# Every second chunk's narrow one-hot on ScalarE, and counts evicted one strip later, in a graph network's counting stage

## The chip, the cores and the metric

The kernel runs on one core of a Trainium2 chip. The metric is the device time of one execution in microseconds (us). Three runs of the kernel before gave 6667.44, 6668.77 and 6669.37 us; the time before is their median, 6668.77 us.

## The reference, cut to what matters

Four graph networks (GIN, SuperGAT, a GCN/GRU chain of four blocks and an edge-filtered update) run one after the other over 3125 nodes and 100000 edges, each followed by a residual sum and a layer norm. The edges are sorted by destination. The part that matters here is the first network's sum over neighbours, which the third network uses again:

```python
edge_index = jnp.stack([src, dst])

def _gin_conv(x, src, dst, W1, b1, W2, b2):
    agg = jax.ops.segment_sum(x[src], dst, num_segments=N_NODES)
    h = x + agg
    h = jnp.maximum(h @ W1 + b1, 0.0)
    return h @ W2 + b2
```

The kernel doesn't gather rows for this. It builds a dense matrix of counts once (how many edges go from node s to node d, plus one on the diagonal for the `x +`), and multiplies by it.

## The kernel before, in words

**The counting stage** is `build_counts`. Nodes are padded to 3200, in 25 tiles (`NT`) of 128; a tile of destinations is cut into 4 strips (`PER`) of 32 destinations (`WIN`), 100 strips in all. Edges come in chunks of 128 and steps of two chunks. For strip w, `bounds` (lines 187 to 190) loads two register values from SBUF: the first step and the end of the steps that touch this strip. Since a step on the border of two strips is done in both, there are 490 steps, so 980 chunks; most strips have 5 steps.

For each chunk VectorE (DVE) makes two one-hot matrices: `pick_lo` (line 250), 128 edges by 128, marks the low 7 bits of the source; `pick_key` (line 251), 128 edges by 800, marks the pair of source tile and destination within the strip. TensorE (PE) multiplies them (line 280): `pick_lo` is the stationary side, `pick_key` the moving one, in two matmuls of 416 and 384 columns, which add into an accumulator in PSUM. Both one-hots have two buffers (b = 0 and 1, the first and second chunk of a step). DVE waits at line 249's `used` until PE has done the chunk two before; PE waits for `picked`. Around a strip PE opens the accumulator with a product of zeros (line 274) and closes it with another (line 284, semaphore `closed`). There are two accumulators; line 273 (`moved`) lets PE open one only when ScalarE (ACT) has evicted the strip two before. ACT evicts a closed strip with two copies (line 261), in the order of the strips, and does nothing else in this stage.

**GpSimd (POOL) has other work in the same block.** It sorts edge rows for the last network (class `Sender`, lines 1656 to 1702): for each tile of the counts it sends 22 chunks by indirect DMA (line 1688), in two halves of 11, each with a copy of the indices (line 1681) and a load of the next rows (line 1670). After its 22 sends, `tile` (lines 206 to 211) waits until all four strips of the tile are evicted (`moved`), and adds the identity to the diagonal block (line 211). The next tile's sends come behind it. A stage ends when all engines have come to its end: `Mem.clear` has barriers, and the next stage (`gin_conv`) begins behind them.

All engines run their own instruction streams, in order, with loops made by `Fori`; the loops over steps have bounds in registers.

Of the kernel before, what the change touches and what calls it, by code (L numbers as in the profile page):

```python
# [12 lines left out]
P = 128  # L13
N_NODES = 3125
NT = -(-N_NODES // P)
# [10 lines left out]
WIN = 1 << WIN_BITS  # L26
NWIN = NP // WIN
PER = P // WIN
# [15 lines left out]
ALU = mybir.AluOpType  # L44
ACT = mybir.ActivationFunctionType
AX_X = mybir.AxisListType.X
ds = bass.ds
# [112 lines left out]
def build_counts(nc, K, D, AT):  # L160

    with ExitStack() as ctx:
        m = Mem(nc, ctx)
        dst = m.sb("b_dst", [P, NC], I32)
        src = m.sb("b_src", [P, NC], I32)
        bits = m.sb("b_bits", [P, NC], I32)  # L170
        lof = m.sb("b_lof", [P, NC + 4 * NWIN])
        keyf = m.sb("b_keyf", [P, NC + 4 * NWIN])
        base = m.sb("b_base", [P, NWIN])
        lane = m.sb("b_lane", [P, KEYS], I16)
        lanef = m.sb("b_lanef", [P, KEYS])
        pick_lo = m.sb("b_pick_lo", [P, 2, P], BF16)
        pick_key = m.sb("b_pick_key", [P, 2, KEYS], BF16)
        zeros = m.sb("b_zeros", [P, BANK], BF16)
        sender = Sender(m, D, "b", *COUNT_SENDS)
        acc = [m.ps(f"b_acc{s}", [P, 2, BANK]) for s in range(2)]  # L180
        loaded, ready, picked, used, closed, moved, diag = (
            m.sem(f"b_{n}") for n in ("loaded", "ready", "picked", "used", "closed", "moved", "diag"))
        halves = ((0, 0, KEYS_L), (1, KEYS_L, KEYS))
        real = slice(2 * NWIN, 2 * NWIN + NC)
        flat = AT[:, :, :].rearrange("p j d -> p (j d)")

        def bounds(eng, w):
            lo = eng.value_load(K["bounds"][0:1, ds(w, 1)], min_val=0, max_val=NSTEP + NWIN)
            hi = eng.value_load(K["bounds"][0:1, ds(w + 1, 1)], min_val=1, max_val=NSTEP + NWIN)
            return lo, hi  # L190

        with nc.Block() as block:
            @block.sync
            def _(sp):
                sp.dma_start(dst[:, :], D["dst_pc"]).then_inc(loaded, 16)
                sp.dma_start(src[:, :], D["src_pc"]).then_inc(loaded, 16)

            @block.gpsimd
            def _(pool):
                pool.iota(lanef[:, :], pattern=[[1, KEYS]], base=0, channel_multiplier=0,  # L200
                          allow_small_or_imprecise_dtypes=True).then_inc(ready, 1)
                pool.iota(base[:, :], pattern=[[KEYSPAN, NWIN]], base=0, channel_multiplier=0,
                          allow_small_or_imprecise_dtypes=True).then_inc(ready, 1)
                sender.begin(pool)

                def tile(t, first):
                    sender.send(pool, t, 0, first)
                    sender.send(pool, t, 1)
                    pool.wait_ge(moved, t * (2 * PER) + 2 * PER + 2)
                    block_ = flat[:, ds(t * (NP + P), P)]  # L210
                    pool.tensor_tensor(block_, block_, K["identb"][:, :], ALU.add).then_inc(diag, 1)
                tile(0, True)
                with pool.Fori(1, NT) as t:
                    tile(t, False)
                pool.wait_ge(diag, NT)
                sender.end(pool)

            @block.vector
            def _(dve):
                dve.memset(zeros[:, :], 0.0)  # L220
                dve.drain().then_inc(used, 2)
                dve.wait_ge(ready, 2)
                dve.tensor_copy(lane[:, :], lanef[:, :])
                dve.wait_ge(loaded, 32)
                dve.tensor_scalar(bits[:, :], src[:, :], P - 1, None, ALU.bitwise_and)
                dve.drain()
                dve.tensor_copy(lof[:, real], bits[:, :])
                dve.drain()
                dve.tensor_scalar(bits[:, :], src[:, :], P_BITS, None, ALU.arith_shift_right)
                dve.drain()  # L230
                dve.tensor_scalar(keyf[:, real], bits[:, :], float(WIN), None, ALU.mult)
                dve.drain()
                dve.tensor_scalar(bits[:, :], dst[:, :], WIN - 1, None, ALU.bitwise_and)
                dve.drain()
                dve.tensor_tensor(keyf[:, real], keyf[:, real], bits[:, :], ALU.add)
                dve.drain()
                dve.tensor_scalar(bits[:, :], dst[:, :], WIN_BITS, None, ALU.arith_shift_right)
                dve.drain()
                dve.scalar_tensor_tensor(out=keyf[:, real], in0=bits[:, :], scalar=float(KEYSPAN), in1=keyf[:, real],
                                         op0=ALU.mult, op1=ALU.add)  # L240
                dve.drain().then_inc(ready, 1)
                with dve.Fori(0, NT) as t:
                    for q in range(PER):
                        w = dve.snap(t * PER + q)
                        lo, hi = bounds(dve, w)
                        with dve.Fori(lo, hi) as n:
                            for b in range(2):
                                c = dve.snap((n - w + NWIN) * 2 + b)
                                dve.wait_ge(used, n * 2 + b + 1)
                                dve.tensor_scalar(pick_lo[:, b, :], lane[:, 0:P], lof[:, ds(c, 1)], None, ALU.is_equal)  # L250
                                dve.tensor_scalar(pick_key[:, b, :], lane[:, :], base[:, ds(w, 1)], keyf[:, ds(c, 1)],  # L251
                                                  ALU.add, ALU.is_equal).then_inc(picked, 1)

            @block.scalar
            def _(act):
                act.sem_inc(moved, 2)
                with act.Fori(0, NT) as t:
                    for q in range(PER):
                        act.wait_ge(closed, t * PER + q + 1)
                        for h, lo, hi in halves:  # L260
                            act.activation(AT[:, lo // WIN:hi // WIN, ds(t * P + q * WIN, WIN)],
                                           acc[q % 2][:, h, 0:hi - lo].rearrange("p (j d) -> p j d", d=WIN),
                                           ACT.Copy).then_inc(moved, 1)

            @block.tensor
            def _(pe):
                pe.wait_ge(ready, 3)
                with pe.Fori(0, NT) as t:
                    for q in range(PER):
                        w = pe.snap(t * PER + q)  # L270
                        lo, hi = bounds(pe, w)
                        pe.wait_ge(moved, w * 2)
                        for h, a, z in halves:
                            pe.matmul(acc[q % 2][:, h, 0:z - a], zeros[:, 0:P], zeros[:, 0:z - a],
                                      start=True, stop=False, skip_group_check=True)
                        with pe.Fori(lo, hi) as n:
                            for b in range(2):
                                pe.wait_ge(picked, n * 2 + b + 1)
                                for h, a, z in halves:
                                    mm = pe.matmul(acc[q % 2][:, h, 0:z - a], pick_lo[:, b, :], pick_key[:, b, a:z],  # L280
                                                   start=False, stop=False, skip_group_check=True)
                                mm.then_inc(used, 1)
                        for h, a, z in halves:
                            mm = pe.matmul(acc[q % 2][:, h, 0:z - a], zeros[:, 0:P], zeros[:, 0:z - a],
                                           start=False, stop=True, skip_group_check=True)
                        mm.then_inc(closed, 1)
# [1819 lines left out]
```

## Time and profile before

| what | value |
|---|---|
| median of three runs | 6668.77 us |
| the profiled execution's own time | 6675.19 us |
| its span | 6673.6 us |
| busy in the span: PE, DVE, ACT, POOL | 4334.3, 3767.7, 1205.4, 3659.2 us |
| counting stage, from 151 to 1019 us | 13% of the span |

The sums and the range below are made on differences from the profiled execution, which took 6675.19 us, 1.6 us more than its span and 6.4 us (0.1%) more than the median. In the rows, times are in us from the span's start; "x2" is the number of instructions merged into a row; what stands in brackets is the idle time of the engine before the row and the engine and line that ended it. A name with a q (DVEq, ACTq, PEldq) is an engine's sequencer: register, load and branch instructions, which are not counted as busy.

### The profile page before, as it was taken

How to read it: one execution, taken by the hardware profiler on the slowest of the kernel's cores; microseconds unless marked ns; L12 is line 12 of the kernel's file. 1: busy time of each engine (PE TensorE's matmuls, PEld its weight loads, DVE VectorE, ACT ScalarE, POOL GpSimd, SP SyncE). 2: the span in 40 equal slices, each digit the busy share in tenths (PEclk: the TensorE clock that was granted, in tenths of full speed). 3: DMA queues.
4: the chain of work that ended last, by engine and by line, in shares of the span. 5: the costliest groups of instructions: out<-in, count | busy, mean ns of one | idle time of the engine just before them, and what ended most of it. 6: DMA issues, size and time to landing. Idle time of an engine off the chain costs nothing. (4 is left out here: it accounts for less than half of the span.)

```text
span 6673.6 us, 101944 instructions
## 1 busy us (share of the span) xinstructions
PE 4334.3 (65%) x26966; PEld 3026.4 (45%) x26967; DVE 3767.7 (56%) x8412; ACT 1205.4 (18%) x2011; POOL 3659.2 (55%) x3721
## 2 busy tenths in 40 slices
PE   0666667186267777775466666641888778778774
PEld 0111114154156566553355555531555556556653
DVE  8777771054589898988466666662111244444443
ACT  0111111011211111111212211110211222222221
POOL 1666664600277777772477777735000057777771
PEclk9999998598589899987577777766998888888886
DMA  4111114110244444443233333353000123222344
GB/s 198 41 44 44 41 44 177 46 33 15 64 127 116 123 122 121 117 123 75 74 81 80 79 80 83 82 114 130 11 18 21 31 64 75 74 75 74 75 71 42
DMA packets 309188, 518.20 MB, mean 78 GB/s; under 512 B 105621, under 2 KB 221727, under 8 KB 298934
## 3 DMA queue, kind: packets, MB, share of 16 engines
q0 software_dynamic: 131616, 291.86, 18.6%
q1 hardware_dynamic: 177430, 224.82, 10.3%
q8 instruction: 43, 0.70, 0.0%
q14 instruction: 99, 0.81, 0.0%
HBM read 412.95 MB, written 103.45 MB: 77 GB/s over the span
## 5 line engine op out<-in xcount | busy, mean ns | idle before, releaser
L1017 POOL DMA_INDIRECT e_ring<-att_rows,e_near x1792 | 1841.6, 1028 | 550.2 <-issue 484.2
L1770 POOL DMA_INDIRECT e_nodes<-x,e_edges x880 | 884.2, 1005 | 311.5 <-issue 274.5
L1084 PE MATMUL e_psum<-e_ring,e_whole_pick 128*128 128x264 f32 (+1 forms) x3584 | 849.5, 390 | 297.8 <-DVE e_ring L1244 288.8
L1084 PEld LDWEIGHTS e_psum<-e_ring,e_whole_pick 128*128 128x128 f32 x3584 | 649.4, 225 | 423.5 <-issue 195.7
L1039 PE MATMUL e_px<-t_parts,e_pick 128*128 x5376 | 692.9, 270 | 118.1 <-DVE e_prod L1162 56.3
L1162 DVE TENSOR_TENSOR e_prod<-e_px,e_ring 128x512 f32<-128x512 f32 x672 | 458.3, 682 | 495.9 <-DMA e_ring<-att_rows,e_near 413.3
L1688 POOL DMA_INDIRECT sorted<-bx_held,bx_index x550 | 545.0, 991 | 251.3 <-issue 248.9
L280 PE MATMUL b_acc<-b_pick_key,b_pick_lo 128*128 128x416 bf16 (+1 forms) x1960 | 504.4, 346 | 176.5 <-DVE b_pick_key L251 159.5
L350 PE MATMUL r_pa<-gru_counts,gru_parts 128*128 x3000 | 448.7, 316 | 187.3 <-DMA r_bh<-in_gru_bh 169.6
L1039 PEld LDWEIGHTS e_px<-t_parts,e_pick 128*128 128x128 bf16 x5376 | 452.6, 107 | 210.2 <-issue 139.5
L1126 ACT ACTIVATE e_whole_pick<-e_pturn 128x512 f32<-128x512 bf16 x448 | 266.5, 595 | 1324.8 <-PE e_pturn L1075 1280.5
L251 DVE TENSOR_SCALAR b_pick_key<-b_lane,b_base,b_keyf 128x800 bf16<-128x800 int16 x980 | 487.4, 497 | 0.0
L1806 PE MATMUL e_pa<-e_msg,e_pick 128*128 128x128 f32 x1768 | 315.6, 333 | 249.4 <-DVEq L1864 248.4
L1806 PEld LDWEIGHTS e_pa<-e_msg,e_pick 128*128 128x128 f32 x1768 | 264.4, 229 | 435.4 <-DVEq L1864 420.4
L350 PEld LDWEIGHTS r_pa<-gru_counts,gru_parts 128*128 128x128 bf16 x3000 | 306.7, 103 | 328.9 <-issue 193.5
L1152 DVE TENSOR_REDUCE e_dots<-e_prod 128x8 f32<-128x512 f32 (+1 forms) x672 | 453.0, 674 | 0.0
L350 PE MATMUL g_pa<-gin_counts,g_parts 128*128 x2250 | 319.6, 306 | 191.8 <-ACT g_parts L316 160.6
L1244 DVE TENSOR_TENSOR e_ring<-e_ring 128x1024 f32<-128x1024 f32 (+1 forms) x448 | 423.7, 946 | 23.7 <-issue 23.7
L250 DVE TENSOR_SCALAR b_pick_lo<-b_lane,b_lof 128x128 bf16<-128x128 int16 x980 | 264.6, 270 | 239.1 <-PE b_acc L280 194.8
L1761 POOL IOTA e_lane<- 128x128 f32 x1 | 0.2, 237 | 712.2 <-ACTq L1822 712.2
L1863 DVE TENSOR_TENSOR e_msg<-e_msg,e_nodes 128x512 f32<-128x512 f32 x220 | 153.7, 699 | 397.3 <-DMA e_nodes<-x,e_edges 395.9
L280 PEld LDWEIGHTS b_acc<-b_pick_key,b_pick_lo 128*128 128x128 bf16 x1960 | 121.5, 98 | 543.5 <-DVE b_pick_key L251 527.7
(335 smaller groups left out, 6579.9 us busy)
## 6 DMA issues: line engine op xcount, KB each, us to landing
e_relb<-place SPq DMA_DIRECT2D x56, 1024.0 KB
sorted<-o_fill SPq DMA_DIRECT2D x13, 2244.0 KB, 34.3
e_edges<-sorted SPq DMA_DIRECT2D x221, 132.0 KB
e_ring<-att_rows,e_near POOLq DMA_INDIRECT x1792
kept<-gin_counts SPq DMA_DIRECT2D x5, 4000.0 KB, 33.5
gru_counts<-kept SPq DMA_DIRECT2D x5, 4000.0 KB
bx_held<-in_edge_rows POOLq DMA_DIRECT2D x51, 363.0 KB
e_nodes<-x,e_edges POOLq DMA_INDIRECT x880
```

Of the source, the lines that this page charges most:

```text
L251: dve.tensor_scalar(pick_key[:, b, :], lane[:, :], base[:, ds(w, 1)], keyf[:, ds(c, 1)], ALU.add, ALU.is_equal).then_inc(picked, 1)
L280: mm = pe.matmul(acc[q % 2][:, h, 0:z - a], pick_lo[:, b, :], pick_key[:, b, a:z], start=False, stop=False, skip_group_check=True)
L350: mm = pe.matmul(banks, parts[:, k, j, f * P:(f + 1) * P], AT[:, j, ds(g * GW + half * HW, HW)], start=(j == 0 and k == 0), stop=(j == NT ...
L1017: pool.indirect_dma_start(out=ring[:, s, r, 0:wd + HEADS], out_offset=None, in_=xrows, in_offset=bass.IndirectOffsetOnAxis(ap=near[:, s, r ...
L1039: mm = pe.matmul(px[g % 2][:, x * wd:(x + 1) * wd], pick[:, 1 - s, r, :], parts[:, n, ds(t, 1), :].rearrange("p o c -> p (o c)"), start=(n ...
L1084: mm = pe.matmul(psum[q % 2][:, 0:RING], whole_pick[:, q % 2, c, :], ring[:, s, q * G + c, :], start=(c == 0), stop=(c == G - 1))
L1152: dve.tensor_reduce(dots[:, s, :, g * XB:(g + 1) * XB].rearrange("p h x -> p x h"), prod[:, g % 4, :].rearrange("p (x h c) -> p x h c", x= ...
L1162: dve.tensor_tensor(prod[:, g % 4, :].rearrange("p (x c) -> p x c", x=XB), px[g % 2][:, :].rearrange("p (x c) -> p x c", x=XB), ring[:, 1 ...
L1244: dve.tensor_tensor(rows_, rows_, ring[:, s, q * G:(q + 1) * G, wd:wd + HEADS].unsqueeze(3).broadcast_to([P, G, HEADS, ch]), ALU.mult).the ...
L1688: pool.indirect_dma_start(out=self.D["sorted"], in_=self.held[s][:, u, :], in_offset=None, out_offset=bass.IndirectOffsetOnAxis(ap=self.in ...
L1770: pool.indirect_dma_start(out=nodes[:, s, u, :], out_offset=None, in_=source, in_offset=bass.IndirectOffsetOnAxis(ap=edges[:, q, u, RBF + ...
L1806: mm = pe.matmul(pa[s][:, 0:P], pick[:, s, u, :], msg[:, s, u, :], start=(u == 0), stop=(u == SUB - 1))
```

## The change

DVE keeps making `pick_key` for both chunks of a step and `pick_lo` for the first one. The `pick_lo` of the second chunk is made by ACT with two activations: the absolute difference of the lane number and the source's low bits, into a new f32 tile `away`, and then relu(1 - that). ACT waits for its own first result (`away_made`), for `used`, and at the end of each step for its own second result (`placed`). PE waits for `placed` as well before the second chunk. ACT now loads the bounds of each strip and loops over its steps. The eviction of a strip comes behind ACT's work for the next strip, in place of right after the strip was closed; the last one comes behind everything.

```diff
+        away = m.sb("b_away", [P, P])
...
                             for b in range(2):
                                 c = dve.snap((n - w + NWIN) * 2 + b)
                                 dve.wait_ge(used, n * 2 + b + 1)
-                                dve.tensor_scalar(pick_lo[:, b, :], lane[:, 0:P], lof[:, ds(c, 1)], None, ALU.is_equal)
+                                if b == 0:
+                                    dve.tensor_scalar(pick_lo[:, b, :], lane[:, 0:P], lof[:, ds(c, 1)], None, ALU.is_equal)
                                 dve.tensor_scalar(pick_key[:, b, :], lane[:, :], base[:, ds(w, 1)], keyf[:, ds(c, 1)],
                                                   ALU.add, ALU.is_equal).then_inc(picked, 1)
...
             def _(act):
                 act.sem_inc(moved, 2)
-                with act.Fori(0, NT) as t:
-                    for q in range(PER):
-                        act.wait_ge(closed, t * PER + q + 1)
-                        for h, lo, hi in halves:
-                            act.activation(AT[:, lo // WIN:hi // WIN, ds(t * P + q * WIN, WIN)],
-                                           acc[q % 2][:, h, 0:hi - lo].rearrange("p (j d) -> p j d", d=WIN),
-                                           ACT.Copy).then_inc(moved, 1)
+                act.wait_ge(ready, 3)
+
+                def place(t, q):
+
+                    w = act.snap(t * PER + q)
+                    lo, hi = bounds(act, w)
+                    with act.Fori(lo, hi) as n:
+                        c = act.snap((n - w + NWIN) * 2 + 1)
+                        act.activation(away[:, :], lanef[:, 0:P], ACT.Abs, bias=lof[:, ds(c, 1)], scale=-1.0).then_inc(away_made, 1)
+                        act.wait_ge(used, n * 2 + 2)
+                        act.wait_ge(away_made, n + 1)
+                        act.activation(pick_lo[:, 1, :], away[:, :], ACT.Relu, bias=1.0, scale=-1.0).then_inc(placed, 1)
+                        act.wait_ge(placed, n + 1)
+
+                def move(t, q):
+                    act.wait_ge(closed, t * PER + q + 1)
+                    for h, lo, hi in halves:
+                        act.activation(AT[:, lo // WIN:hi // WIN, ds(t * P + q * WIN, WIN)],
+                                       acc[q % 2][:, h, 0:hi - lo].rearrange("p (j d) -> p j d", d=WIN),
+                                       ACT.Copy).then_inc(moved, 1)
+
+                def rest(t):
+                    for q in range(1, PER):
+                        place(t, q)
+                        move(t, q - 1)
+                place(0, 0)
+                rest(0)
+                with act.Fori(1, NT) as t:
+                    place(t, 0)
+                    move(t - 1, PER - 1)
+                    rest(t)
+                move(NT - 1, PER - 1)
...
                             for b in range(2):
                                 pe.wait_ge(picked, n * 2 + b + 1)
+                                if b == 1:
+                                    pe.wait_ge(placed, n + 1)
```

## Rows read from the trace of the kernel before

**Rows 1.** Timeline of POOL at the end of the counting stage: its last instruction there.
```profile
1019.36 0.43 POOL L211 TENSOR_TENSOR gin_counts<-gin_counts,identb 128x128 bf16 x1
```
**Rows 2.** Timeline of ACT: evictions, first and second tile, then the last two tiles.
```profile
162.41 0.90 ACT L261 ACTIVATE gin_counts<-b_acc 128x416 f32 x2
...
185.07 0.90 ACT L261 ACTIVATE gin_counts<-b_acc 128x416 f32 x2 [7.48 <-PE b_acc L284]
194.72 1.28 ACT L261 ACT_TABLE_LOAD   x1 [8.75 <-PE b_acc L284]
...
984.74 0.90 ACT L261 ACTIVATE gin_counts<-b_acc 128x416 f32 x2 [7.64 <-PE b_acc L284]
993.70 1.28 ACT L261 ACT_TABLE_LOAD   x1 [8.07 <-PE b_acc L284]
...
1004.37 0.90 ACT L261 ACTIVATE gin_counts<-b_acc 128x416 f32 x2 [1.54 <-PE b_acc L284]
```
**Rows 3.** Timeline of POOL, its diagonal sums alone (25 in the stage).
```profile
186.06 0.62 POOL L211 TENSOR_TENSOR gin_counts<-gin_counts,identb 128x128 bf16<-128x128 bf16 x1 [7.59 <-ACT gin_counts L261]
...
257.06 0.50 POOL L211 TENSOR_TENSOR gin_counts<-gin_counts,identb 128x128 bf16 x1 [1.86 <-ACT gin_counts L261]
290.88 0.51 POOL L211 TENSOR_TENSOR gin_counts<-gin_counts,identb 128x128 bf16 x1
...
985.84 0.50 POOL L211 TENSOR_TENSOR gin_counts<-gin_counts,identb 128x128 bf16 x1 [1.83 <-ACT gin_counts L261]
```
**Rows 4.** Waits from 150 to 1010 us: waiter, releaser, total us, times, longest.
```profile
POOL gin_counts L211 <- ACT gin_counts L261: 24.3, 21, 7.6
```
**Rows 5.** Timeline of DVE and PE: first strip's last chunk, and one later strip.
```profile
160.13 0.11 PEld L280 LDWEIGHTS b_acc<-b_pick_key,b_pick_lo 128*128 128x128 bf16 x2 [0.45 <-DVE b_pick_key L251]
...
505.44 0.48 DVE L251 TENSOR_SCALAR b_pick_key<-b_lane,b_base,b_keyf 128x800 bf16<-128x800 int16 x1
...
507.27 0.25 DVE L250 TENSOR_SCALAR b_pick_lo<-b_lane,b_lof 128x128 bf16<-128x128 int16 x1 [1.34 <-PE b_acc L280]
...
509.54 0.51 PE L280 MATMUL b_acc<-b_pick_key,b_pick_lo 128*128 128x416 bf16 x2 [0.50 <-DVE b_pick_key L251]
...
510.25 0.25 DVE L250 TENSOR_SCALAR b_pick_lo<-b_lane,b_lof 128x128 bf16<-128x128 int16 x1
...
510.42 0.48 DVE L251 TENSOR_SCALAR b_pick_key<-b_lane,b_base,b_keyf 128x800 bf16<-128x800 int16 x1
...
510.95 0.11 PEld L280 LDWEIGHTS b_acc<-b_pick_key,b_pick_lo 128*128 128x128 bf16 x2 [0.57 <-DVE b_pick_key L251]
...
511.66 0.26 DVE L250 TENSOR_SCALAR b_pick_lo<-b_lane,b_lof 128x128 bf16<-128x128 int16 x1
```
**Rows 6.** Line 257 on ACT's sequencer: count, ns (min/median/max), first and last start.
```profile
L257 ACTq ALU_OP  x25: 35/35/35, 185.2 to 1004.5; - x25
...
L257 ACTq FUSED_REGOPS  x24: 50/50/50, 185.4 to 985.1; - x24
```
**Rows 7.** ACT groups by shape: count, busy us, mean ns, idle before.
```profile
L1120 ACT ACTIVATE e_own<-e_diff 128x128 f32<-128x128 f32 x56 | 17.5, 313 | 0.0
L1474 ACT ACTIVATE r_work<-r_work,r_bi 128x640 f32<-128x640 f32 x20 | 16.5, 827 | 22.1 <-DVE r_work L1498 22.1
L316 ACT ACTIVATE gru_parts<-r_work 128x640 bf16<-128x640 f32 x20 | 14.7, 737 | 6.1 <-DVE r_work L332 6.1
```
**Rows 8.** Timeline of ACT where an activation waits for ACT's own activation before it.
```profile
1713.12 0.38 ACT L750 ACTIVATE t_line<-t_pxw 128x256 f32<-128x256 f32 x1 [0.47 <-PE t_pxw L729]
1713.54 1.27 ACT L752 ACTIVATE t_parts<-t_line 128x1280 bf16<-128x1280 f32 x1
```
**Rows 9.** Table loads of ACT: lines 261 and 1832 (the latter in a loop).
```profile
L261 ACT ACT_TABLE_LOAD  x25: 1283/1283/1283, 161.1 to 993.7; - x25
...
L1832 ACT ACTIVATE e_hid<-e_ph,e_b x221: 687/687/688, 5380.9 to 6563.0; 128x512 f32<-128x512 f32 x111
L1832 ACT ACT_TABLE_LOAD  x1: 1283/1283/1283, 5378.8 to 5378.8; - x1
```

More of the change, by code:

```diff
@@ L180, in build_counts @@
         acc = [m.ps(f"b_acc{s}", [P, 2, BANK]) for s in range(2)]
-        loaded, ready, picked, used, closed, moved, diag = (
-            m.sem(f"b_{n}") for n in ("loaded", "ready", "picked", "used", "closed", "moved", "diag"))
+        loaded, ready, picked, placed, away_made, used, closed, moved, diag = (
+            m.sem(f"b_{n}") for n in ("loaded", "ready", "picked", "placed", "away_made", "used", "closed", "moved", "diag"))
         halves = ((0, 0, KEYS_L), (1, KEYS_L, KEYS))
```

## The prediction

> **What bounds the kernel now.** The change touches the counting stage alone, 151 to 1019 us, so I read that stage's end first. POOL's last diagonal sum starts at 1019.36, right behind its last send and with no wait [rows 1]; nothing of the next stage starts before it is done. ACT's last eviction starts at 1004.37 [rows 2]: PE, DVE and ACT had been done for some 14 us. So the stage ends with POOL. Next, what POOL does: 25 tiles of 22 sends, each tile ended by a diagonal sum. From the first sum (186.06) to the last (1019.36) are 833.3 us, 34.72 per tile [rows 1, 3]. Where a tile's sum has no wait, the tile took 33.82 us (257.06 to 290.88) [rows 3], and two more like it took 33.80 and 34.07; the last one, beside idle engines, 33.52 us (985.84 to 1019.36) [rows 1, 3]. Everything above that is POOL waiting for an eviction: 24.3 us in 21 waits, 7.6 of them at the first tile [rows 4]. **Two chains of almost equal length run side by side**: POOL's sends, 33.8 us a tile, and the strips of DVE and PE, on which POOL waits a little at nearly every tile. Even strips that cost nothing could give back no more than those 24.3 us.
>
> Now the strips. Within a strip of 5 steps the busy shares mislead: DVE looks like the bound, but a loop through two buffers is. DVE starts `pick_lo` at 510.25, `pick_key` 0.17 later, and that one takes 0.48; PE loads the chunk's weights at 510.95, 0.05 after its end. PE's two matmuls take 0.51, and 0.20 after such a pair ends (509.54 + 0.51) DVE starts the next `pick_lo` for the buffer that it frees (510.25). The loop is 0.17 + 0.48 + 0.05 + 0.51 + 0.20 = 1.41 us, and two chunks on, at 511.66, DVE is indeed 1.41 later [rows 5]. It holds for each of the two buffers. DVE's own work on two chunks is 2 x (0.17 + 0.48) = 1.30 at most, since its instructions overlap a little. So a step takes 1.41, and DVE has 0.1 to spare. At the tile's start a strip of 5 steps takes 8.96 us (its end at 993.70 against 984.74 before), within a tile 8.54 (984.74 less the 7.64 idle and the 0.90 of the eviction before) [rows 2]; I reckon with 8.47, the commonest in the stage. What is not steps is mostly the loading of the bounds: DVE's last key starts at 505.44, the next strip's first instruction at 507.27 [rows 5], 1.83 us later.
>
> **The change, part by part.**
>
> *DVE loses `pick_lo` of the second chunk*, 490 times. The first chunk's loop keeps all its terms, so a step still takes 1.41. What is gained is the end of a strip: the second chunk's key starts 0.17 earlier (the distance of lo and key [rows 5]), so the last chunk, the closing, and on DVE the loading of the next bounds come 0.17 earlier. That is 0.17 per strip, 16.5 us over the 97 strips up to the last but one diagonal sum.
>
> *ACT makes it instead.* Durations: a 128x128 activation without a pointer takes 0.31 us; a per-partition bias costs 827 - 737 = 90 ns [rows 7]. Abs with the pointer bias: 0.40. Relu with bias 1.0: 0.31, or 0.40 if that constant is read from memory; I take 0.31, since no row here shows a constant bias costing anything. ACT waiting for its own result costs 1713.54 - 1713.50 = 0.04 [rows 8]; with a second wait in the queue, 0.06. From the end of Relu to the next Abs: wait 0.04, then count, branch and registers, which on ACT's tile loop go from 185.2 to 185.4 plus 0.05, 0.25 to 0.27 [rows 6], then the chunk's address and the start, some 0.15: 0.46 in all. One cycle: 0.40 + 0.06 + 0.31 + 0.46 = 1.23 us, 0.18 under the step. Nothing proves these gaps for this loop: 0.60 is the other bound. Beside DVE's key (0.48) the Relu (0.31 to 0.40), released by the same `used`, is hidden.
>
> *Between strips* ACT leaves the loop (0.3), starts the eviction, and its sequencer loads the next bounds behind it. DVE needs 1.83 from its last key to the next strip; ACT's branch is already in the 0.3, so I take 1.7, in all 2.0 from the last Relu to the next Abs. Then a strip costs ACT 5 x 0.77 + 4 x 0.46 + 2.0 = 7.7 us; with the dear Relu 8.1. Both are under 8.3, what DVE and PE then need (8.47 - 0.17). **ACT stays just off the path, by 0.2 to 0.6 us per strip.** Upper bound: Relu 0.40, 0.46, and 2.5 between strips: 8.64.
>
> *Table loads.* Before, ACT reloads its table at each turn of the tile loop, 25 times, since the first turn enters without one; where code ahead of a loop had set it, as at line 1832, one load serves 221 activations [rows 9]. In the changed kernel the first strip's step loop is entered without a table: 5 loads in its 5 steps, none later. A step there costs ACT 1.28 + 1.23 = 2.51. The first Relu ends near 154.0, the fifth at 164.0, while that strip's last chunk started at 160.13 before [rows 5]: 3.9 us late. A load at 161.1 that takes 1.283 [rows 9] is followed at once by the eviction at 162.41 [rows 2]. The Trainium skill ("ScalarE: Activation LUTs", What ACT_TABLE_LOAD costs) gives 2.66 us for a switch, with a drain of 1.38; by that, 5 loads would cost 6.9 us more and the time would be 6671 us. No drain is seen between these rows, so I leave it out.
>
> *The eviction comes a strip later.* PE doesn't notice: strip w + 1 needs strip w - 1 moved, which is done 1.2 us after the last Relu of strip w (0.3 + 0.90), while PE still has a chunk, the closing and its own bounds ahead of it, over 2 us by DVE's 1.83. **But POOL waits for it.** The first sum, at 186.06, needed the eviction that started at 185.07 [rows 2, 3]. Now that one starts behind strip 4's Relus. Strip 4 closed before at 194.72 [rows 2]; its last chunk starts 0.96 earlier (as 160.13 before 161.1 [rows 5, 9]), the Relu ends 0.05 before: 193.7. Plus 0.3, 0.9 and 0.2 to POOL: 195.1. Less 5 x 0.17, plus 3.9: 198.2, so 12.1 us later than now. In the same way the sum of the last but one tile, 985.84, now hangs on the strip that closed at 993.70: 993.70 - 1.01 + 1.4 = 994.1, 8.25 later.
>
> *POOL and its queue.* Its instructions don't change. POOL's sends behind a late sum come late too, and nothing makes up for it.
>
> *Small things.* PE's extra wait per step stands at the second chunk, which has 0.17 to spare: nothing; if that is used up, 490 x 0.04 = 20 us. Two more semaphores and 64 KB of SBUF: nothing. SP has no instruction moved.
>
> **The sum.** Last but one diagonal sum: 985.84 + 3.9 + 8.25 - 97 x 0.17 = 981.5. POOL alone, from its first sum: 198.2 + 23 x 33.9 (the unwaited tiles, rounded up) = 977.9, so the strips set it still. The last tile's sends behind it, 33.52: 1015.0 against 1019.4. **4.4 us less**, since what the strips gain, the late first and last evictions take back. The profiled execution would be 6670.8; against the median, 6.4 lower, 6664.4 us.
>
> **The rivals.** *ACT becomes the bound* (slower). A strip at 8.64 in place of 8.47: 985.84 + 12.15 + 97 x 0.17 + 33.52 = 1048, 28.6 us more: 6697 us. With 0.60 in place of 0.46 per step it is 9.2 us a strip and some 80 us more, 6750. It decides from the point where ACT's strip passes 8.3; it costs time from 8.35 on. For it: the chain of ACT is serial, four waits a step, no slack between strips. Against it: each term above from a row. Chance 0.33.
>
> *POOL is the floor, and is itself a little faster* with DVE less busy. Strips quick enough: 198.2 + 24 x 33.9 = 1011.8, 7.6 less. With the undisturbed 33.52 throughout: 1002.7, 16.7 less, 6652 us. For it: sends last longer beside a busy DVE than in the last tile. Against it: DVE stays busy for 1.2 of 1.4 us. Chance 0.20, of which 0.15 more than 0.2%.
>
> *A table load in every step.* Then ACT's strip is 5 x 2.05 + 4 x 0.46 + 3.28 = 15.4 us, and the time grows by (15.4 - 8.47) x 97 = 670, to about 7350 us. The loop at line 1832 speaks against it: 221 activations, one load [rows 9]. Chance 0.03. The Trainium skill ("ScalarE activation tables: per-element evaluation and per-set limits", Table sets in the compiler and the runtime) says that the loads are placed per block; by that rule each turn of the step loop would have one, and this rival's time would come. The trace disagrees there.
>
> *The sum as worked out, near no change:* 0.44.
>
> **How the numbers follow.** A measurement of this kernel can tell about 0.2%, 13 us, from no change. The forecast and the milder part of POOL as floor fall within that: 0.44 + 0.05 = 0.49. Faster by more: 0.15. Slower: ACT as bound and the table loads, 0.36. Range: down to the undisturbed POOL, 6650; up past ACT at 8.64, to 6706. ACT at 9.2 and the tables lie outside. The likeliest case's own range is 6658 to 6673.
>
> **What would show it.** Right: 5 table loads on ACT in this stage, all before 165 us; Abs near 0.40 and Relu 0.31; the first diagonal sum near 198; few waits of POOL afterwards; PE's steps still 1.4 us. DVE's `pick_lo` 490 times in place of 980. Wrong: PE's second chunk waiting for ACT's Relu (then ACT bounds), strips over 8.5, diagonal sums more than 34.7 apart; or a stage shorter than 850 us, which would mean that the loop through the buffers isn't what holds the steps.

## The result, and the profile after

The changed kernel is slower: 6688.32 us (median of 8 runs, 6683.09 to 6698.37) against 6669.89 us for the kernel before on the same chips; ratio 1.0028, 95% interval 1.0017 to 1.0039. Run again beside more runs of both it was 6693.62 against 6677.11 us, ratio 1.0024 (1.0015 to 1.0033). The prediction was 6664.4 us and "no change". The measured time lies in the range of 6650 to 6706 us, but on the slower side.

| | before | after | after, again |
|---|---|---|---|
| the profiled execution's time, us | 6675.19 | 6683.09 | 6705.03 |
| first diagonal sum | 186.06 | 196.80 | 196.30 |
| last diagonal sum | 1019.36 | 1028.37 | 1031.13 |
| per tile from first to last | 34.72 | 34.65 | 34.78 |
| closing of the last strip | 1003.74 | 1002.03 | 997.89 |
| mean length of a send | 0.991 | 1.009 | 1.013 |

The end of the counting stage on POOL, a timeline (answers to [rows 1]):

```profile
1026.13 0.95 POOL L1717 DMA_INDIRECT sorted<-bx_held,bx_index  x1 [0.30 <-issue]
1027.39 0.96 POOL L1717 DMA_INDIRECT sorted<-bx_held,bx_index  x1 [0.30 <-issue]
1028.37 0.44 POOL L212 TENSOR_TENSOR gin_counts<-gin_counts,identb 128x128 bf16 x1
```

POOL still ends the stage, 9.0 us later than before, and again without a wait. The diagonal sums, first two and last three (answers to [rows 3]):

```profile
196.80 0.42 POOL L212 TENSOR_TENSOR gin_counts<-gin_counts,identb 128x128 bf16<-128x128 bf16 x1 [17.34 <-ACT gin_counts L276]
232.45 0.42 POOL L212 TENSOR_TENSOR gin_counts<-gin_counts,identb 128x128 bf16 x1 [0.26 <-ACT gin_counts L276]
...
959.55 0.43 POOL L212 TENSOR_TENSOR gin_counts<-gin_counts,identb 128x128 bf16 x1
994.50 0.63 POOL L212 TENSOR_TENSOR gin_counts<-gin_counts,identb 128x128 bf16 x1
1028.37 0.44 POOL L212 TENSOR_TENSOR gin_counts<-gin_counts,identb 128x128 bf16 x1
```

And POOL's waits for evictions (total us, times, the longest), 24.3 us in 21 before [rows 4]:

```profile
POOL gin_counts L212 <- ACT gin_counts L276: 17.6, 2, 17.3
```

POOL waits for 17.3 us at the first tile, for 0.26 at the second, and then never again. So by all that was argued it should have made its tiles in 33.9 us each. It made them in 34.65. **That is where the forecast failed: POOL, whose instructions didn't change, got slower by 0.7 us per tile**, and 24 tiles make 18 us.

The groups of the stage's middle, 200 to 980 us (name, shape, count, busy us, mean ns, idle before and what ended it), show the new work on ACT and the slower sends:

```profile
L1717 POOL DMA_INDIRECT sorted<-bx_held,bx_index x496 | 501.3, 1011 | 231.0 <-issue 222.1 <-DMA bx_held<-in_edge_rows 4.6 <-ACT gin_counts L276 4.3
L267 ACT ACTIVATE b_away<-b_lanef,b_lof 128x128 f32<-128x128 f32 x453 | 181.8, 401 | 206.9 <-ACT b_pick_lo L270 144.9 <-issue 62.0
L270 ACT ACTIVATE b_pick_lo<-b_away 128x128 bf16<-128x128 f32 x453 | 140.1, 309 | 144.8 <-PE b_acc L309 140.6
```

A send took 991 ns on the mean before in the same stretch. **The mean hides two kinds of sends.** Each send (count, then the shortest, the median and the longest in ns, then the first and last start in us), before and after:

```profile
L1688 POOL DMA_INDIRECT sorted<-bx_held,bx_index x495: 954/972/1182, 199.8 to 979.2; - x165
...
L1717 POOL DMA_INDIRECT sorted<-bx_held,bx_index x496: 954/972/1205, 199.1 to 979.6; - x166
```

The median is the same. What grew is the number of long ones: of the sends that began between 200 and 980 us, 42 of 494 took 1060 ns or more before and 131 of 495 after, 1.10 and 1.11 us on the mean, while the others took 0.98 in both. Of the 131, 129 began while DVE was making a wide key, and none of the 231 that began while DVE was idle was long. The disturbance goes both ways: 127 of DVE's wide keys took over 580 ns (the median is 482), and during every one of them an instruction of POOL ended (during 40% of all its 905 keys there).

One step of DVE and ACT in the timeline (answers to [rows 5]):

```profile
503.50 0.25 DVE L252 TENSOR_SCALAR b_pick_lo<-b_lane,b_lof 128x128 bf16<-128x128 int16 x1 [0.37 <-PE b_acc L309]
503.67 0.88 DVE L253 TENSOR_SCALAR b_pick_key<-b_lane,b_base,b_keyf 128x800 bf16<-128x800 int16 x2
503.89 0.31 ACT L270 ACTIVATE b_pick_lo<-b_away 128x128 bf16<-128x128 f32 x1 [0.32 <-PE b_acc L309]
...
504.60 0.40 ACT L267 ACTIVATE b_away<-b_lanef,b_lof 128x128 f32<-128x128 f32 x1 [0.40 <-ACT b_pick_lo L270]
...
504.92 0.25 DVE L252 TENSOR_SCALAR b_pick_lo<-b_lane,b_lof 128x128 bf16<-128x128 int16 x1 [0.37 <-PE b_acc L309]
```

The step is still 1.42 us (503.50 to 504.92). What is new on DVE is the pair: two wide keys run without a break for 0.88 us, then DVE idles for 0.37. Before, narrow and wide alternated.

### The profile page after: what moved, and what is told of

Read it like the earlier page. It is cut to its first block and busy times, and to the rows that moved or that the text cites. A ratio compares the mean times of both kernels' runs of the same rounds, so it can differ in the third digit from the quotient of the medians.

```text
span 6681.5 us, 105599 instructions
## 1 busy us (share of the span) xinstructions
PE 4303.2 (64%) x26966; PEld 3029.2 (45%) x26967; DVE 3696.5 (55%) x7922; ACT 1527.9 (23%) x2972; POOL 3671.5 (55%) x3721
## 5 line engine op out<-in xcount | busy, mean ns | idle before, releaser
L309 PE MATMUL b_acc<-b_pick_key,b_pick_lo 128*128 128x416 bf16 (+1 forms) x1960 | 481.8, 345 | 193.1 <-DVE b_pick_key L253 186.9
L253 DVE TENSOR_SCALAR b_pick_key<-b_lane,b_base,b_keyf 128x800 bf16<-128x800 int16 x980 | 454.8, 504 | 2.1 <-PE b_acc L309 2.1
L379 PEld LDWEIGHTS g_pa<-gin_counts,g_parts 128*128 128x128 bf16 x2250 | 222.1, 99 | 301.2 <-issue 211.6
```

The lines of the kernel that those rows point to most:

```text
L379: mm = pe.matmul(banks, parts[:, k, j, f * P:(f + 1) * P], AT[:, j, ds(g * GW + half * HW, HW)], start=(j == 0 and k == 0), stop=(j == NT ...
```

## The experiments

Three theories for POOL's slower tiles. **ACT**: its 980 new activations (two for each of 490 steps) slow the others through memory. **DVE's pattern**: two wide keys back to back hold a send up longer than two with a narrow one between. **Free running**: before, POOL began each tile in step with the strips and so met DVE at the same harmless moments; without the wait it doesn't.

**e1_again.** No edit.

> The changed kernel once more, with a second profile. In the first one, GpSimd's tiles of 22 sends, which no longer wait for ScalarE, took 34.65 us each from the first diagonal sum to the last (before: 33.8 to 34.1 where unwaited, 34.72 with waits), and the stage's last sum came at 1028.4 in place of 1019.4. All theories expect the same again: first sum near 197, tiles of 34.5 to 35, kernel 13 to 25 us over the kernel before. If the tiles come out at 33.9 here, the slower sends were chance, and the cost must be sought outside the stage.

The numbers are in the table above: first sum 196.30, tiles of 34.78, sends of 1.013 us. The slower sends are no chance.

**e2_act_beside.** ACT works, but for nobody.

```diff
+        spare_lo = m.sb("b_spare_lo", [P, P], BF16)
...
-                                if b == 0:
-                                    dve.tensor_scalar(pick_lo[:, b, :], ...)
+                                dve.tensor_scalar(pick_lo[:, b, :], ...)
...
-                        act.activation(pick_lo[:, 1, :], away[:, :], ACT.Relu, ...)
+                        act.activation(spare_lo[:, :], away[:, :], ACT.Relu, ...)
...
-                                if b == 1:
-                                    pe.wait_ge(placed, n + 1)
```

> ScalarE does all its new work, but into a spare tile; VectorE makes every narrow one-hot as before and TensorE doesn't wait for ScalarE's. The output is right. Theory ScalarE (its two activations per step slow GpSimd's sends and VectorE through memory): sends longer than 1.00 us on the mean, unwaited tiles 34.6 or more, keys over 0.500 us. Theory VectorE's pattern (two wide keys back to back, with no narrow one between, hold GpSimd up longer) and theory free running (beside strips that set its pace GpSimd meets VectorE at the same harmless moments in every tile): sends at 0.99, unwaited tiles 33.8 to 34.1. In all of them the strips don't gain 0.17 each while the eviction still comes a strip late, so the last but one sum moves 8.25 us back: by the last two theories some 8 us more than before (6677), by the first more than that.

Measured: 6680.99 us, ratio 1.0009 (0.9999 to 1.0018). First sum 194.46, last 1022.23, 34.49 per tile with five small waits in it. The same stretch of 200 to 980 us:

```profile
L1715 POOL DMA_INDIRECT sorted<-bx_held,bx_index x498 | 498.7, 1001 | 230.3 <-issue 228.2 <-DMA bx_held<-in_edge_rows 1.8 <-ACT gin_counts L276 0.3
```

This met neither expectation: 1001 ns lies between before (991) and after (1011), and the tiles without a wait, but for the last one, took 34.1 to 34.8 us. The 2.9 us at the last sum are less than the 8 that the late eviction alone was to cost. ACT's work costs a send 10 ns at most here.

**e3_dve_less.** DVE's new stream without ACT's new work. It leaves out the narrow one-hot of every second chunk, so the counts of those chunks are missing.

```diff
+                dve.memset(pick_lo[:, :, :], 0.0)
                 dve.drain().then_inc(used, 2)
...
-                                dve.tensor_scalar(pick_lo[:, b, :], ...)
+                                if b == 0:
+                                    dve.tensor_scalar(pick_lo[:, b, :], ...)
```

> The kernel before, but the narrow one-hot of the second chunk isn't made at all (its buffer is zero), so half the counts are left out; ScalarE evicts as before and has no new work. VectorE's stream is the changed kernel's. Theory ScalarE: GpSimd's tiles take 33.9 us; the strips gain 0.17 each, the last sum comes at 1003 and the kernel takes 16 us less, 6653. Theory VectorE's pattern: tiles 34.65, last sum near 1017, 2 us less, 6667. Theory free running: the strips are now quicker than the sends, so GpSimd waits no longer, and the tiles take 34.65 too, 6667; it is the next run that tells it from VectorE's pattern.

Measured: 6687.49 us, ratio 1.0015 (1.0006 to 1.0024). So leaving out 490 instructions of DVE and adding nothing made the kernel slower. First sum 185.90, last 1022.89, 34.87 per tile, and only the first one waited:

```profile
L1690 POOL DMA_INDIRECT sorted<-bx_held,bx_index x491 | 502.4, 1023 | 228.1 <-issue 220.2 <-DMA bx_held<-in_edge_rows 7.0 <-ACT gin_counts L263 0.9
```

Sends of 1023 ns with ACT at its evictions alone: theory ACT falls as the main cause. The strips, on the other hand, did what was predicted of DVE's relief: the last one closed at 985.74, 18.0 us earlier, 0.18 for each of 100. The kernel's 10 us are more than the 3.5 at the last sum; see what stays open.

**e4_before_late_sum.** The kernel before, with POOL's diagonal sum a tile late.

```diff
                 def tile(t, first):
                     sender.send(pool, t, 0, first)
                     sender.send(pool, t, 1)
+
+                def diagonal(t):
                     pool.wait_ge(moved, t * (2 * PER) + 2 * PER + 2)
...
                 with pool.Fori(1, NT) as t:
                     tile(t, False)
+                    diagonal(t - 1)
+                diagonal(NT - 1)
```

> The kernel before, but GpSimd adds the diagonal of tile t-1 behind the sends of tile t, so that it waits for no eviction until the end. VectorE's and ScalarE's work is unchanged. Theories ScalarE and VectorE's pattern: the sends of a tile take 33.9 us, GpSimd is through with them near 992 and waits for the last strips (1005.3): last sum near 1006, 13 to 14 us less than before, 6656. Theory free running: 34.65 us per tile once GpSimd no longer starts each tile in step with the strips; last sends end near 1010, last sum near 1011, 8 to 9 us less, 6661.

Measured: 6663.09 us, ratio 0.9979 (0.9969 to 0.9989). POOL's waits are gone, up to one of 3.5 us at the very end. The sends from 200 to 980 us:

```profile
L1692 POOL DMA_INDIRECT sorted<-bx_held,bx_index x503 | 499.4, 993 | 231.2 <-issue 226.9 <-DMA bx_held<-in_edge_rows 4.3
```

and its end, a timeline:

```profile
1000.09 0.43 POOL L213 TENSOR_TENSOR gin_counts<-gin_counts,identb 128x128 bf16 x1
1004.00 0.42 POOL L213 TENSOR_TENSOR gin_counts<-gin_counts,identb 128x128 bf16<-128x128 bf16 x1 [3.48 <-ACT gin_counts L265]
```

POOL runs free here, and the sends stay at 993 ns; the tiles take 34.25 us (212.41 to 1000.09, 23 of them). Against the 33.9 of the few tiles that had no wait before, free running costs 0.35 us per tile; the other 0.40 of the changed kernel's 34.65 comes with DVE's pattern, and 22 sends of 15 ns more each (1.009 against e4's 0.994) make 0.33 of it. **The kernel takes 14 us less than before: this version beats both kernels.**

**e5 to e8.** These four ran where the kernel before itself took 7677.33 us (24 executions, 7640 to 7718), so they are told only for what is seen there.

**e5_after_late_sum.** The edit of e4, on the changed kernel.

```diff
                 def tile(t, first):
                     sender.send(pool, t, 0, first)
                     sender.send(pool, t, 1)
+
+                def diagonal(t):
                     pool.wait_ge(moved, t * (2 * PER) + 2 * PER + 2)
...
                     tile(t, False)
+                    diagonal(t - 1)
+                diagonal(NT - 1)
```

> The changed kernel, with the diagonal of tile t-1 added behind the sends of tile t, so that the eviction that comes a strip later holds nobody up. Theory two costs (the changed kernel pays about 10 us once for the late first eviction, and about 0.6 us per tile for slower sends): the once-paid part goes, the sends run from 147 us on at 34.7 per tile and are through near 1012, last sum near 1013, so 15 to 18 us under the changed kernel, 6 to 7 under the kernel before, and some 8 over the kernel before with the same edit. If the last sum comes near 1004 here, the slower sends were an effect of waiting late and not of VectorE's pattern.

**e6_narrow_between.** On the changed kernel: the narrow one-hot stands between the two wide keys again.

```diff
+                                key = dve.tensor_scalar(pick_key[:, b, :], ...)
                                 if b == 0:
-                                    dve.tensor_scalar(pick_lo[:, b, :], ...)
-                                dve.tensor_scalar(pick_key[:, b, :], ...).then_inc(picked, 1)
+                                    key = dve.tensor_scalar(pick_lo[:, b, :], ...)
+                                key.then_inc(picked, 1)
```

> The changed kernel with one edit: VectorE makes the wide key of the first chunk before its narrow one-hot, so that the narrow one lies between the two wide ones. Same instructions, same number. Theory VectorE's pattern: sends back to 0.99 to 1.00 us, tiles to 34.1 to 34.3, last sum at 197 + 24 x 34.2 = 1018, so 10 us under the changed kernel and about level with the kernel before. Theory that VectorE's idle gaps decide (the sum of its idle time is the same, one gap per step, only shifted): sends stay at 1.010 and tiles at 34.7.

**e7_table_first.** On the changed kernel: one Abs ahead of the loops.

```diff
                 act.wait_ge(ready, 3)
+                act.activation(away[:, :], lanef[:, 0:P], ACT.Abs)
+                act.drain()
```

> The changed kernel with one activation ahead of ScalarE's loops, which loads the table once. No load in the first strip's steps (5 before). First strip's last chunk some 3 us earlier, first diagonal sum at 193 to 194 in place of 196.6; as GpSimd alone sets the rest, the whole stage and kernel 2 to 4 us shorter than the changed kernel.

**e8_evict_own.** On the changed kernel: ACT evicts a strip before the next one's steps.

```diff
-                    for q in range(1, PER):
+                    for q in range(PER):
                         place(t, q)
-                        move(t, q - 1)
-                place(0, 0)
+                        move(t, q)
                 rest(0)
                 with act.Fori(1, NT) as t:
-                    place(t, 0)
-                    move(t - 1, PER - 1)
                     rest(t)
-                move(NT - 1, PER - 1)
```

> The changed kernel, but ScalarE evicts a strip right behind its own steps, and not a strip later. Theory two costs: first sum near 189, 7 to 8 us earlier, and if the strips stay quicker than the sends (34.7 per tile) the last sum comes near 1022, 7 us under the changed kernel. Rival: ScalarE now waits for the closing before its next bounds, some 2.5 us between its last Relu and the next Abs plus the closing, so it is late for each strip's first step by 0.6 us or more; strips of 8.7 or more set the pace, GpSimd waits at each tile again and the last sum comes at 1030 or later.

Against that 7677.33 us: e5 7611.17 (ratio 0.9911, 0.9879 to 0.9943), e6 7747.22 (1.0096, 1.0068 to 1.0124), e7 7628.07 (0.9935, 0.9915 to 0.9955), e8 7702.04 (1.0035, 1.0013 to 1.0058). None of the expectations on POOL's tiles could be tried. What e7 was to do on ACT it did: one table load ahead of the loops and none in them, and the first strip's fifth Relu ended at 159.50 and not at 162.28 as in the changed kernel. In e5, from 200 to 980 us, the strips got through 1441 of the chunks' matmuls where the same kernel got through 1816 elsewhere (e9); each took 407 ns and not 341 (granted clock of this stretch 0.78 against 0.99), and PE and DVE idled more for "issue", in which they waited for nothing that the profile shows (DVE before its narrow one-hot for 94.2 us, against 18.2 in e9; PE before these matmuls for 52.5, against less than 1):

```profile
L313 PE MATMUL b_acc<-b_pick_key,b_pick_lo 128*128 128x384 bf16 (+1 forms) x1441 | 425.9, 407 | 228.1 <-DVE b_pick_key L257 168.3 <-issue 52.5 <-ACT b_pick_lo L274 4.1
...
L256 DVE TENSOR_SCALAR b_pick_lo<-b_lane,b_lof 128x128 bf16<-128x128 int16 x359 | 102.3, 285 | 317.8 <-PE b_acc L313 211.0 <-issue 94.2 <-remote 11.7
```

Why that is so on this chip wasn't tried. POOL waited at nearly every tile (waits of e5 over the whole stage):

```profile
POOL gin_counts L214 <- ACT gin_counts L280: 203.4, 22, 13.6
```

Here the strips set the stage, by far, and there the changed kernel with its table loaded first is faster than the kernel before by 0.65%. The changed kernel itself wasn't run there, so that its own ratio is about this is argued from e7 (one table load ahead of the loops in place of five in them) and not shown.

**e9_after_late_sum_2.** e5's kernel, beside a kernel before of 6678.01 us.

> The same kernel as e5_after_late_sum, once more, since e5 to e8 ran where the kernel before itself took 7677 us and the strips, not the sends, set the stage. If the kernel before takes some 6670 us here: last sum near 1013, 6 to 7 us under the kernel before, by theory two costs; near 1004 if VectorE's pattern doesn't slow the sends. If it takes 7600 again: as e5, under the kernel before by 0.9%, since there the strips are the bound.

Measured: 6671.34 us, ratio 0.9991 (0.9981 to 1.0000), 6.7 us under the kernel before. The end of the stage:

```profile
1009.29 0.97 POOL L1721 DMA_INDIRECT sorted<-bx_held,bx_index  x1 [0.30 <-issue]
1010.29 0.81 POOL L214 TENSOR_TENSOR gin_counts<-gin_counts,identb 128x128 bf16 x2
```

The last sums come at 1010.29, with sends of 1010 ns and 34.62 us per tile. Against the changed kernel (1028.4, 1031.1) that is 18 to 21 us less: the 17.3 of the first wait. Against the same edit on the kernel before, 1004.00, it is 6.3 more: the slower sends (which cost more than that, since POOL had 3.5 us to wait at the end there).

**e10_narrow_between_2.** e6's kernel, beside 6678.01 us.

> The same kernel as e6_narrow_between, once more, for the same reason. Beside a kernel before of some 6670 us: theory VectorE's pattern says sends of 0.99 to 1.00 us, tiles of 34.1 to 34.3, last sum near 1018, kernel about level with the kernel before; theory idle gaps says sends of 1.010, tiles of 34.7, 15 us over the kernel before.

Measured: 6735.18 us, ratio 1.0087 (1.0070 to 1.0104). The sends are short again (e10, the groups from 200 to 980 us):

```profile
L1718 POOL DMA_INDIRECT sorted<-bx_held,bx_index x472 | 466.9, 989 | 218.1 <-issue 213.2 <-DMA bx_held<-in_edge_rows 4.9
```

at 989 ns, with the same instructions as in the changed kernel and ACT at work. That speaks for DVE's pattern; but POOL waited here too, so by this run alone it could be free running (e11 parts the two). And the kernel is 57 us slower than before and not level with it, since the strips became the bound: POOL waited 74.1 us in 23 waits, the last strip closed at 1047.08. DVE's timeline shows why:

```profile
501.38 0.49 DVE L251 TENSOR_SCALAR b_pick_key<-b_lane,b_base,b_keyf 128x800 bf16<-128x800 int16 x1 [0.55 <-PE b_acc L310]
501.78 0.25 DVE L254 TENSOR_SCALAR b_pick_lo<-b_lane,b_lof 128x128 bf16<-128x128 int16 x1
501.94 0.48 DVE L251 TENSOR_SCALAR b_pick_key<-b_lane,b_base,b_keyf 128x800 bf16<-128x800 int16 x1
...
502.88 0.53 DVE L251 TENSOR_SCALAR b_pick_key<-b_lane,b_base,b_keyf 128x800 bf16<-128x800 int16 x1 [0.45 <-PE b_acc L310]
```

A step is 1.50 us (501.38 to 502.88). PE begins the first chunk 0.70 after DVE, as before, and takes 0.51 (from 502.09); the key then starts 0.28 after PE's end and not 0.20. DVE is idle for 0.45 of the 1.50, so it isn't DVE's work that makes the step: it is the loop through the first chunk's buffer, and 0.08 more in it are 0.08 more per step.

**e11_between_late.** Both edits.

> The changed kernel with both edits: the narrow one-hot between the wide ones, and the diagonal added a tile late. Theory two costs, each edit takes away one of them: sends of 34.2 per tile from 147 us on are through near 1000, the last strips near 1003, last sum near 1004, 14 to 16 us under the kernel before, at or just under the kernel before with the late sum alone (14 under).

Measured: 6714.77 us, ratio 1.0048 (1.0031 to 1.0065); the expectation was missed for the reason of e10, which was not known yet. The tiles before the strips hold POOL up are of use: from the first sum to the sixth, five of them took 34.18, 34.43, 34.16, 33.90 and 33.88 us, 34.11 on the mean, where e9 has 34.62. POOL waits for nothing in these tiles of either, and the kernels differ in the order of two instructions, and by it in the step (1.50 against 1.42 us): theory DVE's pattern stands. The longer step means 6% fewer keys per us; that this makes the difference is spoken against by e3 and e4, which differ as much with steps of 1.42 and 1.41 us.

**e12_evict_own_2.** e8's kernel, beside 6670.60 us.

> The same kernel as e8_evict_own, once more, beside a kernel before of some 6670 us, if it comes to that. The same expectations: first sum near 189; last sum near 1022 and the kernel 7 us under the changed one if the strips stay quicker than the sends; 1030 or later, with GpSimd waiting for evictions again, if ScalarE, which then starts each strip's bounds only behind the closing of the one before, is late for the first step of every strip. After e10 (a first chunk's path longer by 0.08 us made every step longer by as much) I expect the second, strips of 8.8 to 9.0 us, and a last sum near 1045.

Measured: 6700.04 us, ratio 1.0044 (1.0028 to 1.0061). First sum 189.07, as foretold; then 35.45 us per tile, waits of 24.7 us in 12 included, to the last sum at 1039.93. The strips took 8.72 us (median) where they have 5 steps (8.51 in the changed kernel), and PE waited 350 times for ACT's Relu, so ACT does hold them up, but they closed at 1025.55 and again POOL ended the stage, with sends of 1.021 us. The late eviction is the better order of the two; what it costs is the first wait. Why the sends are slower still here wasn't tried.

Side by side, by what DVE's order is and whether ACT makes one-hots (mean of all the stage's sends, in e11 too):

| kernel | DVE's keys | ACT's one-hots | mean send, us | us per tile |
|---|---|---|---|---|
| before | with a narrow one between | no | 0.991 | 34.72, waits in it |
| e4 | with a narrow one between | no | 0.994 | 34.25 |
| e2 | with a narrow one between | yes, spare | 1.001 | 34.49, small waits in it |
| e10 | with a narrow one between | yes | 0.990 | 36.36, waits in it |
| e11, first five tiles, without wait | with a narrow one between | yes | 0.989 | 34.11 |
| e3 | in pairs | no | 1.021 | 34.87 |
| changed, twice | in pairs | yes | 1.009, 1.013 | 34.65, 34.78 |
| e9 | in pairs | yes | 1.010 | 34.62 |
| e12 | in pairs | yes | 1.021 | 35.45, waits in it |

The traces show the same send by send. Of the sends from 200 to 980 us that began while DVE was making a wide key, this many took 1060 ns or more: with a narrow one-hot between the keys 42 of 342 (before), 51 of 328 (e4), 78 of 344 (e2), 49 of 242 (e10) and 45 of 257 (e11); in pairs 129 of 170 and 137 of 186 (changed, twice), 159 of 221 (e3), 118 of 159 (e9) and 156 of 301 (e12). Of those that began beside an idle DVE, 122 to 238 in each kernel, none did.

## Why the prediction was wrong, step by step

- **The bound.** Right: POOL ends the stage, before and after, and strips alone could give back little. e4 took the waits away and gained 14 us, a little over half of the 24.3.
- **The step through two buffers, 1.41 us.** Right: 1.42 in the changed kernel, though DVE does 490 instructions less, and e10 lengthened the loop and got the step that follows from it. The gain of 0.17 per strip was right as well (0.18 in e3).
- **ACT's durations.** Right: Abs 401 ns (0.40 in the sum), Relu 309 (0.31), from Relu's end to the next Abs 0.40 (0.46), five table loads. A step with a load took 2.40 us (153.05 to 155.45 at line 267) and one without 1.13 (163.74 to 164.87): a load costs its own 1.28 and no drain. That ACT stays off the path was at most half right. Strips of 5 steps took 8.51 us (median) as before, and not 8.3; without ACT's part (e3) they took 8.37. The last strip closed only 2 to 6 us earlier and not 12.6, and in e3 18.0: PE waited for ACT's Relu 79 times for 32.5 us in the first profile and 61 times for 26.4 in the second, a wait that the sum had at nothing. Nothing came of it for the stage, as POOL was behind anyway.
- **The late eviction.** Right: first sum 196.80 (198.2 in the sum), 10.7 us later than before.
- **POOL's queue.** Wrong, and it is the step that failed. "*Its instructions don't change*" is true, and "POOL alone, from its first sum: 198.2 + 23 x 33.9" took their duration for fixed. The term was mis-sized by 0.75 us per tile: 24 x 34.65 = 832 from 196.80 gives the 1028.4 that was measured, where the prediction's way gives at most 1015. By e4, 0.35 of the 0.75 isn't DVE's pattern: 33.9 was read off the three tiles before the last that had no wait, and a POOL that waits at no tile takes 34.25 beside the old pattern. The other 0.40 came with the new one, 0.33 of it in the sends. Nor was "few waits of POOL afterwards" a sign that the sum was right: it came true and the tiles were longer all the same. The sum said -4.4 us at the end of the stage; it was +9.0, and +11.8 in the second profile.
- **The rivals.** "POOL is the floor, and is itself a little faster" had the mechanism and the wrong sign: DVE did less work and POOL got slower. "ACT becomes the bound" was given 0.33, and nearly all the chance of "slower" was put on it; the kernel got slower, but not by it. The table load in every step didn't come.

**What stays open.** The last sum explains 9.0 and 11.8 us of a median difference of 16 to 18. In the two profiles the first network's own part, from the last diagonal sum to the last instruction on `g_y`, took another 2.7 and 4.4 us more than before (605.1 and 606.9 against 602.5). It took 605.6, 606.2 and 603.8 in e2, e3 and e4, and 602.5 and 602.9 in e9 and e11. What moves it, and what the rest is, wasn't settled. Nor do the runs show by which path DVE's keys hold the sends up. The Trainium skill ("GPSIMD Engine Reference", Key points) says that GpSimd shares its interfaces to SBUF with VectorE and contends with some of its modes. The trace agrees in so far as sends take 0.960 us beside an idle DVE (the last eleven, in both kernels) and 0.989 to 1.021 beside a busy one.

## What to carry to other kernels

When two chains of nearly equal length run side by side, price the change on both, and don't take the other chain's durations for constants: its engine may share something with the one whose stream is rearranged. Where an engine waits for a result that nobody needs yet, move the wait behind its next block of work first; here that gave 14 us at no cost, more than any redistribution of the one-hots. Look at how single durations are spread before you call an engine slower: here most sends kept their length, and more of them became long. And a busy share of 0.72 on the busiest engine (DVE before, from 200 to 980 us) is no reason to unload it: look for the loop through the buffers, and for the term in it that the change really shortens.

## What the runs showed of the hardware that was not expected

- The order of DVE's instructions, not their amount, set the pace of POOL's indirect sends: in the pairs of runs that differ in it, two wide keys (0.88 us for the pair) back to back cost a send 8 to 27 ns on the mean (1.009 against e2's 1.001, e9's 1.010 against e11's 0.989, e3's 1.021 against e4's 0.994), and leaving 490 narrow instructions out made the sends longer.
- A send that began during a wide key took over 1060 ns in 12 to 23% of the cases where a narrow one-hot stands between the keys, and in 52 to 76% where they run in pairs; a send that began beside an idle DVE never did.
- DVE's first instruction of a step started 0.20 us after PE's end where it is the narrow one-hot, which reads one column at a computed address, and 0.28 where it is the key, which reads two (e10). Whether the addresses make the difference wasn't tried.
- The same kernel took 6670 to 6678 us beside the other runs and 7677 beside e5 to e8, where the strips set the stage (granted clock from 200 to 980 us 0.78 in e5, 0.99 for the same kernel in e9). There an edit of the changed kernel was faster than the kernel before (e7, 0.9935), which it may well not be elsewhere (not shown).
